# One transformer layer on one core: sums of the first normalisation on ScalarE, banks emptied ahead of the diagonal, and several steps in other slots

## The reference

```python
x = x + attention(layernorm(x))      # 16 heads of 16 channels
x = x + (h @ W.T + b + (h @ V_r) @ C.T)   # h = layernorm(x), rank 32
```

## Time and profile before

| | |
|---|---|
| median of three runs | 2274.64 us (2272.21 to 2276.3) |
| profiled execution, its own time | 2274.01 us |
| its span, first to last instruction | 2272.7 us |
| mean granted TensorE clock | 0.978 of full speed |
| TensorE / VectorE / ScalarE / GpSimd busy | 94% / 87% / 61% / 51% |
| ScalarE waiting for the diagonal (L673 for L539) | 601.0 us in 820 times |
| GpSimd waiting for the first or second statistics (L739 for L516) | 378.9 us in 63 times |

### The profile page before, as it was taken

One profiled execution on the slowest core, in us unless ns is written; L12 is line 12 of the kernel. 1 busy time (PEld: TensorE's weight loads), 2 busy tenths in 40 slices (PEclk: granted clock), 3 DMA queues, 4 the chain that ended last, 5 costly groups with the idle time before them and its releaser, 6 DMA issues. The chain is left out here.

```text
span 2272.7 us, 77397 instructions
## 1 busy us (share of the span) xinstructions
PE 2140.8 (94%) x31524; PEld 1130.2 (50%) x31524; DVE 1980.0 (87%) x5949; ACT 1383.4 (61%) x1666; POOL 1151.2 (51%) x966
## 2 busy tenths in 40 slices
PE   3899999999999999999999999999999999999996
PEld 1245555555555555555545555555555555555553
DVE  5599999999998989999989999998999999999972
ACT  0166666666666666666666666666666666666662
POOL 3436555554545545555555455555545555554421
PEclk8699999999999999999999999999999999999997
DMA  5323433333333332343333333333333333323310
GB/s 117 110 77 87 117 84 106 110 85 99 105 107 87 105 108 77 105 115 87 102 111 85 99 105 110 86 107 114 85 100 105 108 87 106 115 79 104 97 32 24
DMA packets 158868, 218.49 MB, mean 96 GB/s; under 512 B 19024, under 2 KB 104912, under 8 KB 158512
## 3 DMA queue, kind: packets, MB, share of 16 engines
q1 hardware_dynamic: 157232, 211.44, 32.9%
q10 hardware_dynamic: 1280, 2.10, 0.3%
HBM read 36.52 MB, written 16.78 MB: 23 GB/s over the span
## 5 line engine op out<-in xcount | busy, mean ns | idle before, releaser
L529 DVE CUSTOM_DVE_ANT_0 junk<-ps_s,alibi 128x512 bf16<-128x512 f32 x2048 | 1323.5, 683 | 191.7 <-PE ps_s L364 155.3
L673 ACT ACTIVATE pt<-ps_t 128x1024 f32<-128x1024 f32 x1024 | 1050.8, 1026 | 606.1 <-DVE ps_t L539 601.0
L364 PE MATMUL ps_s<-at 64*128 64x512 f32 x2048 | 817.5, 462 | 20.6 <-DVE row_max L529 9.7
L372 PE MATMUL ps_t<-at 64*128 64x512 f32 x2048 | 776.3, 453 | 1.2 <-ACT pt L673 1.2
L385 PE MATMUL ps_o<-pt,v_one 128*17 128x128 f32 x16384 | 642.5, 275 | 2.9
L385 PEld LDWEIGHTS ps_o<-pt,v_one 128*17 128x17 f32 x16384 | 424.0, 98 | 328.3 <-issue 220.7
L539 DVE SCALAR_TENSOR_TENSOR ps_t<-diag,slope,ps_t 128x256 f32<-128x256 f32 x1024 | 495.4, 484 | 27.6 <-PE ps_t L372 27.6
L364 PEld LDWEIGHTS ps_s<-at 64*128 64x128 f32 x2048 | 331.4, 186 | 294.2 <-DVE row_max L529 215.3
L802 POOL TENSOR_TENSOR rope_a<-rope_a,swapped 128x512 f32<-128x512 f32 x128 | 161.6, 1284 | 469.5 <-DMA swapped<-rope_b 469.5
L372 PEld LDWEIGHTS ps_t<-at 64*128 64x128 f32 x2048 | 326.4, 185 | 33.2 <-ACT pt L673 26.0
L335 PE MATMUL ps_misc<-xt,wqkv_t 128*32 128x512 f32 x2048 | 279.6, 620 | 13.8 <-DVE x L563 6.0
(11 more groups left out here) (72 smaller groups left out, 1447.8 us busy)
## 6 DMA issues: line engine op xcount, KB each, us to landing
at<-halves SPq DMA_DIRECT2D x192, 512.0 KB, 5.1
swapped<-rope_b SPq DMA_DIRECT2D x256, 128.0 KB, 2.6
x_in<-in_L_attn_x_dram SPq DMA_DIRECT2D x32, 512.0 KB, 3.9
num<-o_sb SPq DMA_DIRECT2D x512, 32.0 KB, 2.0
x_res<-in_L_attn_x_dram SPq DMA_DIRECT2D x32, 512.0 KB, 4.2
out_dram<-x_hat SPq DMA_DIRECT2D x32, 512.0 KB, 5.9
at<-spread_den SPq DMA_DIRECT2D x60, 64.0 KB
at<-max_t ACTq DMA_DIRECT2D x128, 16.0 KB
```

The costliest lines, as they stand in the source:

```text
L364: pe.matmul(ps_s[:, t % 2, :], operand(n, 0)[:, t * P:(t + 1) * P], operand(n, 1), start=True, stop=True).then_inc(s_done, 1)
L372: pe.matmul(ps_t[:, j, :], operand(n, 1)[:, j * P:(j + 1) * P], operand(n, 0), start=True, stop=True).then_inc(t_done, 1)
L529: dve.tensor_tensor_reduce(junk[:, t % 2, :], ps_s[:, t % 2, :], alibi[:, off:off + N], 1.0, LOWEST, ALU.add, ALU.max, row_max[:, hb % 2, ...
L673: act.activation(pt[:, h % 2, 2 * pair:2 * pair + 2, :], ps_t[:, 2 * pair:2 * pair + 2, :], ACT.Exp).then_inc(exp_done, 1)
```

## The change

- The first normalisation's sums leave VectorE. ScalarE takes minus the mean (`take_mean`, an activation Copy with scale -1/256 and a running sum) and the sum of squares about it (`take_squares`, Square with the mean as bias), each four times a batch: in slot begin -19 mean 0 and 1 ahead of the first exponential and square 0 ahead of the second; at -18 square 1 and mean 2, then mean 3; at -17 squares 2 and 3 ahead of the first exponential. Their full-size output goes into x_hat, which is overwritten later, so ScalarE now waits for the store.
- GpSimd makes deviation and centring at -17 and the last product (`normalise1`) at -16, and the factor 16 that the sum of squares leaves out is put in where ScalarE copies the turned x_hat (`ROOT_C`).
- VectorE does the divisions and the additions that empty the bank ahead of the diagonal. The second statistics are one group of tokens in each half at 35 and 36. The reciprocals come at 29, second half, and 30, first half.
- TensorE turns the first x_hat at -15 only, a half of the channels in each half; the second QK chunk goes from -9 to -11; the second normalisation's GpSimd part goes from 36 to 37 and behind the rope products, its turning from 38 to 39, the addition of the ffn bias from 38 to 40; the spread of denominators stands ahead of the weighted values.
- SyncE stores at 43 instead of 44, thus in slot 11 of 16, after the x load and ahead of the clearing and the stack.
- The constants' memsets go from VectorE to GpSimd.

```diff
-QK_BEGIN = (-12, -9, -5, -2)
+QK_BEGIN = (-12, -11, -5, -2)
...
 # TensorE
-                    for kc in range(KC):
-                        b = batch_at(slot, (-16, -15)[kc])
-                        if b is not None and half == 0:
-                            turn_tokens("xt", b, kc, x_hat, xhat_done, b + 1, xt_done)
-                    b = batch_at(slot, 38)
+                    b = batch_at(slot, -15)
+                    if b is not None:
+                        turn_tokens("xt", b, half, x_hat, xhat_done, b + 1, xt_done)
+                    b = batch_at(slot, 39)
                     if b is not None:
                         turn_tokens("x2t", b, half, x_hat2, xhat_done2, b + 1, x2t_done)
                     if hb is not None and half == 1:
                         max_rows(hb)
+                    b = batch_at(slot, 31)
+                    if b is not None:
+                        spread_denominators(b, half)
                     if nv is not None:
                         weighted_values(nv, 2 * half)
                         weighted_values(nv, 2 * half + 1)
-                    b = batch_at(slot, 31)
-                    if b is not None:
-                        spread_denominators(b, half)
 # VectorE
-                    if nt is not None:
-                        diagonal_bias(nt, half)
                     b = batch_at(slot, 31)
                     if b is not None:
                         divide(b, half)
...
                         b = batch_at(slot, 41 + u)
                         if b is not None and half == 1:
                             add_linear("ffn", b, u, y, y, x1_biased, y_done)
-                    b = batch_at(slot, -19)
-                    if b:
-                        if half == 0:
-                            dve.wait_ge(x_loaded, 16 * (b + 1))
-                            ln_stats(b, x_in, 0, bn_done, (0, 1))
-                        else:
-                            ln_stats(b, x_in, 0, bn_done, (2, 3))
-                            ln_mean_var(b, 0, bn_done, aggr_done)
-                    b = batch_at(slot, 30)
-                    if b is not None:
-                        denominators(b, half)
+                    if nt is not None:
+                        diagonal_bias(nt, half)
+                    for u in range(2):
+                        b = batch_at(slot, 35 + u)
+                        if b is not None:
+                            ln_stats(b, 2 * u + half)
+                        if b is not None and u == 1 and half == 1:
+                            ln_mean_var(b)
+                    for part in range(2):
+                        b = batch_at(slot, (29, 30)[part])
+                        if b is not None and half == 1 - part:
+                            denominators(b, part)
 # ScalarE
+            def take_mean(b, t):
+                if t == 0:
+                    act.wait_ge(x_loaded, 16 * (b + 1))
+                    if b >= 4:
+                        act.wait_ge(stored, 16 * (b - 3))
+                act.activation(x_hat[:, t, :], x_in[:, t, :], ACT.Copy, scale=-1.0 / C,
+                               accum_out=minus_mean[:, t:t + 1]).then_inc(mean_done, 1)
+
+            def take_squares(b, t):
+                act.wait_ge(mean_done, T * b + t + 1)
+                act.activation(x_hat[:, t, :], x_in[:, t, :], ACT.Square, bias=minus_mean[:, t:t + 1],
+                               accum_out=squares[:, t:t + 1]).then_inc(squares_done, 1)
...
+                b = batch_at(slot, -19)
+                if b:
+                    take_mean(b, 0)
+                    take_mean(b, 1)
+                b = batch_at(slot, -18)
+                if b:
+                    take_squares(b, 1)
+                    take_mean(b, 2)
+                b = batch_at(slot, -17)
+                if b:
+                    take_squares(b, 2)
+                    take_squares(b, 3)
...
                 if nt is not None:
                     exponentials(nt, 0)
...
+                b = batch_at(slot, -19)
+                if b:
+                    take_squares(b, 0)
+                b = batch_at(slot, -18)
+                if b:
+                    take_mean(b, 3)
 # GpSimd
+            def deviation1(b):
+
+                pool.wait_ge(squares_done, T * (b + 1))
+                pool.tensor_tensor(var_eps[:, 0, :], squares[:, :], eps[:, 0, :], ALU.add).then_inc(veps_done, 1)
...
                 hb = half_at(slot, 8)
                 if hb is not None:
                     split_max(hb)
-                b = batch_at(slot, -18)
+                b = batch_at(slot, -16)
                 if b:
-                    inverse_deviation(b, 0, aggr_done, veps_done, rstd_done)
...
+                    normalise1(b)
+                b = batch_at(slot, -17)
+                if b:
+                    deviation1(b)
+                    centre1(b)
                 cc = chunk_at(slot, 1)
...
+                b = batch_at(slot, 37)
+                if b is not None:
+                    normalise2(b)
...
-                b = batch_at(slot, 38)
+                b = batch_at(slot, 40)
 # SyncE
-                b = batch_at(slot, 44)
+                b = batch_at(slot, 43)
```

More of the change, by code:

```diff
@@ L136, in layer @@
         x2t = x_in[:, :, :].rearrange("p a b -> p (a b)").rearrange("p (k n) -> p k n", k=KC)
[L137 to L138 removed]
+        minus_mean = sb("minus_mean", [P, T])
+        squares = sb("squares", [P, T])
+        stats = sb("stats", [P, T, 6])
+        mean_var = sb("mean_var", [P, T, 2])
         var_eps = sb("var_eps", [P, 2, T])
@@ L624, in vector_program @@
                             add_linear("proj", b, u, x1, x_res, res_biased, x1_done)
[L625 to L630, removed]
                         b = batch_at(slot, 41 + u)
@@ L674, in exponentials @@
                                ACT.Exp).then_inc(exp_done, 1)
+            for t in range(T):
+                take_mean(0, t)
+            for t in range(T):
+                take_squares(0, t)
             act.wait_ge(weights_turned, 1)
@@ L680, in scalar_program @@
                 nt = head_at(slot, T_LAG)
[L681 to L685, removed]
-                if bx is not None:
-                    act.wait_ge(xhat_done, min(bx + 4, NB))
-                    copy_turned("x2t", bx, 0, x2t, x2t_done)
+                b = batch_at(slot, -19)
[10 more added lines that the diff above has]
+                    take_squares(b, 3)
+                bx = batch_at(slot, -15)
+                if bx is not None:
+                    copy_turned("xt", bx, 0, xt, ROOT_C, xt_done)
+                b2 = batch_at(slot, 39)
+                if b2 is not None:
+                    act.wait_ge(xhat_done, min(b2 + 4, NB))
+                    copy_turned("x2t", b2, 0, x2t, 1.0, x2t_done)
                 if nt is not None:
@@ L720, in scalar_program @@
                     exponentials(nt, 1)
+                hb = half_at(slot, 8)
                 if hb is not None:
@@ new lines, in centre1, with normalise1, normalise2 @@
+            def centre1(b):
+                pool.wait_ge(rstd_done, b + 1)
+                pool.tensor_tensor(x_hat[:, :, :], x_in[:, :, :], over_channels(minus_mean[:, :]),
+                                   ALU.add).then_inc(centred, 1)
+            def normalise1(b):
+                pool.wait_ge(centred, b + 1)
+                pool.tensor_tensor(x_hat[:, :, :], x_hat[:, :, :], over_channels(rstd[:, 0, :]),
+                                   ALU.mult).then_inc(xhat_done, 1)
+            def normalise2(b):
+                pool.wait_ge(aggr_done, b + 1)
+                pool.tensor_tensor(var_eps[:, 1, :], mean_var[:, :, 1], eps[:, 1, :], ALU.add).then_inc(veps_done2, 1)
+                pool.wait_ge(veps_done2, b + 1)
+                pool.tensor_tensor(rstd[:, 1, :], var_eps[:, 1, :], minus_half[:, :], ALU.pow).then_inc(rstd_done2, 1)
+                pool.wait_ge(rstd_done2, b + 1)
+                pool.tensor_tensor(x_hat2[:, :, :], x1[:, :, :], over_channels(mean_var[:, :, 0]),
+                                   ALU.subtract).then_inc(centred2, 1)
+                pool.wait_ge(centred2, b + 1)
+                pool.tensor_tensor(x_hat2[:, :, :], x_hat2[:, :, :], over_channels(rstd[:, 1, :]),
+                                   ALU.mult).then_inc(xhat_done2, 1)
@@ L763, in split_max @@
                 pool.tensor_tensor(dst[:, :, :, 1, :], src, dst[:, :, :, 0, :], ALU.subtract).then_inc(max_split, 1)
+            pool.memset(minus_half[:, :], -0.5)
+            pool.memset(eps[:, 0, :], C * EPS)
+            pool.memset(eps[:, 1, :], EPS)
+            pool.memset(ones[:, :], 1.0).then_inc(constants, 1)
             pool.memset(v_one[:, :, :, :, :], 1.0)
-            inverse_deviation(0, 0, aggr_done, veps_done, rstd_done)
-            normalise(0, x_in, x_hat, 0, rstd_done, centred, xhat_done)
+            pool.wait_ge(constants, 1)
+            deviation1(0)
+            centre1(0)
+            normalise1(0)
```

64 lines of the change are left out of this document (22 added, 42 removed).

## The result

The changed kernel takes 2400.24 us (median of 4, 2397.84 to 2402.72), the kernel before 2273.43 (2263.48 to 2276.3, 4 runs on the same chip): ratio 1.0566, interval 1.0532 to 1.0600. That is 127 us slower, or 4.2 us for each of some 30 repeating batches, where the prediction had 0.9, and it lies outside the range of 2225 to 2340.

A forecast was written before the change was run, and what follows sets the result against it. The prediction took the bound to change hands between TensorE and VectorE, half by half. Its terms, -2.6 + 2.8 + 0.1 + 0.6 = +0.9 us a batch, times 30, gave 2274 + 27 = 2301 us, range 2225 to 2340.

The forecast's parts named there:

- The gains: Work and waits removed, mainly in slots 13 and 14, slots 5 to 7 and the bank; taken at 2.6 us a batch.
- The sums on slots 13 and 14: First normalisation's statistics leave VectorE, shortening slots 13 and 14 from 9.50 us; gain 1.1 us a batch.
- Slots 5 to 7: TensorE's wait for the second x_hat goes, shortening 11.72 us; gain 1.3 less 0.2, 1.1 us a batch.
- The bank: VectorE empties banks before the diagonal: gain 0.4 us in slots 10 and 11, cost 0.1; slots 3 and 4 hidden.
- ScalarE: Eight added activations in slots 13 to 15, 0.5 us each, load 4 us; nothing directly on the path.
- that rival: ScalarE's squares and exponentials share no table: two loads of 1.28 us per group of squares, 2421 us; chance 0.02.
- The slot 0 wait: TensorE asks for split maxima at 6.5 us, ready at 9.2; wait 2.7, cost taken at 2.8 us a batch.
- The denominators: VectorE waits 1.5 us for them after slot 13's last diagonal, the store freeing 1.7; counted 0.6 us a batch.
- denominators as late as now: Rival in which the reordered store frees nothing for the denominators' transfer: +2.5 us a batch, 2349 us; chance 0.10.
- The sum: All terms per batch: -2.6 + 2.8 + 0.1 + 0.6 = +0.9 us, times 30 = +27 us.
- The other side: Rival that TensorE's slot 0 wait does not bite: -2.0 us a batch, 2214 us, 2196 with both waits gone; chance 0.17.

The follow-up runs named there:

- e9: Changed kernel with GpSimd's rope ahead of deviation and centring, and the two clearing transfers behind the last denominators and numerators on SyncE's queue; 2211.11 us, ratio 0.9734.
- e11: e9 plus four throw-away statistics and four aggregations on VectorE in slot 13; 2238.44 us, ratio 0.9864.
- e10: e9 with VectorE adding the diagonal's bias ahead of the divisions and bank-emptying additions again; 2227.64 us, ratio 0.9807.
- e6: Changed kernel with the two clearing transfers moved from ahead of the stack to behind slot 12's denominators and numerators; 2314.49 us, ratio 1.0196.
- e4: Kernel before with only the reciprocals moved, to 29, second half, and 30, first half; 2336.63 us, ratio 1.0284.
- e2: Changed kernel with GpSimd's rope products ahead of deviation and centring in slot 15; 2328.40 us, ratio 1.0227.
- e1: Changed kernel with the reciprocals put back to begin 30, both halves; 2330.28 us, ratio 1.0258.
- e3: Changed kernel with both edits of e1 and e2: reciprocals back at 30, rope ahead of the centring; 2245.13 us, ratio 0.9869.
- e7: e1 plus twelve throw-away transposes on TensorE in slot 0, ahead of its wait for the split maxima; 2294.93 us, ratio 1.0108.
- e8: e2 with the last group's denominators issued by ScalarE behind the exponential of slot 11; 2219.38 us, ratio 0.9773.

## Why the prediction was wrong, point by point

- **The gains** were forecast at 2.6 us a batch. e9, which has them with neither wait, is 60 us (0.0266 x 2272) under before, 2.0 a batch; by the mean length of a batch from batch 6 to 26 it is 66.90 - 64.54 = 2.4. So somewhat too high. The sums on slots 13 and 14: 1.1 forecast, 0.98 measured (e11); against before itself, slots 13 to 15 together are 1.0 shorter in e9. Slots 5 to 7: 1.1 forecast, 11.71 - 10.94 = 0.8 measured. The bank: 0.3 net forecast, 0.55 measured against the full order of before (e10), with slot 3 wrongly called hidden (4.77 us in e10, 4.52 in e9). Against before itself slot 3 gained nothing (4.48 there); slots 10 and 11 gained 0.24 each.
- **ScalarE** was right. By shape, all in after:

```profile
L656 ACT ACTIVATE x_hat<-x_in,minus_mean 128x256 f32<-128x256 f32 x128 | 64.3, 506 | 0.0
...
L651 ACT ACTIVATE x_hat<-x_in 128x256 f32<-128x256 f32 x128 | 52.3, 410 | 3.0 <-DMA x_in<-in_L_attn_x_dram 3.0
...
L656 ACT ACTIVATION_READ_ACCUMULATOR x_hat<-x_in,minus_mean 128x1 f32 x128 | 24.9, 195 | 0.0
L651 ACT ACTIVATION_READ_ACCUMULATOR x_hat<-x_in 128x1 f32 x128 | 24.6, 192 | 0.0
L651 ACT ACT_TABLE_LOAD x1 | 1.3, 1283 | 0.7 <-PEq L984 0.7
```

  The sum's readout is an instruction of its own, but it overlaps: what follows starts 0.49 us after a square and 0.40 after a mean (medians), 3.6 us a batch where 4 was taken. One table load serves squares and exponentials; that rival is out. The prediction's estimate by the price in the Trainium skill (ScalarE: Activation LUTs, What ACT_TABLE_LOAD costs), 0.40 for a square without its sum, had the overlap taken off; the trace agrees, as the readout starts 0.40 us after its square.
- **The slot 0 wait** had its mechanism and its chain right. In e6, undisturbed by the denominators, the maxima are split 9.16 us after the last diagonal of slot 14 (1079.14 to 1088.30), forecast 9.2. TensorE asks at 7.2 rather than 6.5, so it waits 2.1 (63.1 us in 30) and not 2.7. The rows, a score matmul of before first, then e6:

```profile
1057.46 0.50 PE L364 MATMUL ps_s<-at 64*128 64x512 f32 x1
```

```profile
1079.14 0.48 DVE L543 SCALAR_TENSOR_TENSOR ps_t<-diag,slope,ps_t 128x256 f32<-128x256 f32 x1
1079.37 0.49 PE L368 MATMUL ps_s<-at 64*128 64x512 f32 x1
...
1082.04 0.20 POOL L773 TENSOR_TENSOR var_eps<-squares,eps 128x4 f32<-128x4 f32 x1 [11.72 <-ACT x_hat L656]
...
1088.05 0.25 POOL L811 TENSOR_TENSOR max<-row_max,max 128x32 f32<-128x32 f32 x1
...
1088.44 0.60 PE L399 MATMUL ps_misc<-ident,max 128*16 128x128 f32 x4 [2.07 <-POOL max L811]
```

  TensorE's own way from those scores to its asking did shorten by the turning, from 7.65 us (to 1065.11) to 7.00. But the diagonal that the count starts from stood 0.48 us behind the scores before (1057.94) and stands 0.23 ahead of them now, since VectorE, relieved, waits for TensorE in these halves (0.39 us in the one that follows). What the step left out is the clock behind the wait. Its whole cost, e6 to e9, is 0.0462 x 2272 = 105 us, 3.5 a batch, against 2.8 forecast: 2.1 for the wait, 1.2 for the clock (1.3 in all but two of e6's batches), and 0.2 not assigned.
- **The denominators: here the prediction failed**, twice. First, in "The store now goes ahead of the stack ... so its issue and its data leave the way: between 0 and 3.2 us sooner, taken at 1.7". They freed nothing: the stack's issues grew, and the wait is 2.96, near the 3.2 I had worked out for the transfer left as it was. That was the rival "denominators as late as now", given 0.10; its 2349 us is still 51 too few. Second, in "TensorE has two score banks of lead and ScalarE's lateness overlaps, so I count 0.6 on the end, between 0 and 2.2". TensorE had little lead: of VectorE's 3.16 us in the batch shown it stood for 2.40 at L368, and the half grew from 2.10 (e9) to 4.97 in the median, nearly the whole wait. Where the clock fell behind it, it cost 1.6 us more: the four halves from there on, less VectorE's wait, take 10.4 us in the mean of 13 batches with a fall and 8.8 in each of 14 without (e4: 10.9 in 7, 9.3 in 20). Together the denominators cost, from e2 to e9, 0.0493 x 2272 = 112 us, 3.7 a batch. My bound of 2.2 was no bound.
- **The sum.** Together the waits cost 0.0832 x 2272 = 189 us (after to e9), 6.3 a batch, less than 105 + 112, since the two overlap in part. Less gains of 2.0 that is 4.3. The sum had 3.5 less 2.6. Of the 3.4 missing, 2.8 lie in the waits, most of it in the denominators' 0.6, and 0.6 in the gains.
- **The clock** was in no term and no rival. The rows of before could hardly price it: TensorE's longest regular wait there was 0.67 us in the mean, and its clock never fell between 150 and 2150 us. But the prediction forecast a wait of TensorE several times longer than that in every batch and treated it as idle time alone; that should have widened the range upward.
- **The other side** (2196 us with both waits gone) was the right size for a kernel that e9 comes near to, at 2211, by two changes of order.

## What to carry to other kernels

Before work is moved ahead, find what its input waits for: here the reciprocals ran into a transfer issued 10.5 us down a queue, and in the kernel before that move alone cost 64 us (e4), while on time it was worth at most 16. A wait of TensorE can also cost what its clock loses behind it, here 1.3 to 1.6 us a fall, and a forecast needs a term for that, with a chance of its own. When a change with good parts is slower, look for small pieces ahead of the late producer in its own queue: two clearing transfers and one GpSimd step decided 189 us.

## What the runs showed of the hardware

- Behind a wait of TensorE its clock could go to 1.2 GHz, for 3.4 us or twice that. The length of the wait did not settle it: between 150 and 2150 us it fell behind 27 of e6's 29 waits of 2.07 us and 20 of e1's 25 of 1.65, but behind 7 of e4's 28, which lasted 2.1 in the mean and up to 2.84 without a fall. What else decides is not shown. In e3 VectorE still waited 1.1 us in each of 29 batches and TensorE 0.5 in each of 30, and there was one such stretch, as in e9; in e7 and e8 there was none. A stretch of 3.4 us cost 1.3 us (e6) to 1.6 us (after, e4).
- SyncE's issues are not of fixed length. The same three stack transfers took 6.92, 7.50, and, with the clearing behind them, 3.29 us, part of which was waiting; where the store's issue shrank from 1.31 to 0.51 us, the stack's grew.
- An activation with a running sum is two instructions, 506 + 195 ns for a square of 128x256, and what follows starts 0.49 us after its start.
